# Delta loop of a small hybrid network: order of TensorE's work in a step, two-step loop body, identity products left out

## The reference, cut to what matters

```
def step(S, xs):
    qc, kc, vc, bc = xs
    kb = kc * bc[:, None]
    A = jnp.tril(kb @ kc.T, -1)
    U = solve_triangular(eye + A, vc * bc[:, None] - kb @ S, lower=True)
    o = qc @ S + jnp.tril(qc @ kc.T) @ U
    return (S + kc.T @ U, o)
```

## Time and profile before

| | us |
|---|---|
| median of three runs | 882.79 (877.17 to 887.01) |
| profiled execution, its own time | 882.23 |
| its span | 880.5 |
| TensorE busy | 637.1 (72%) |
| VectorE busy | 440.9 (50%) |
| ScalarE busy | 323.9 (37%) |
| GpSimd busy | 330.2 (38%) |
| mean granted TensorE clock | 0.832 |

### The profile page before, as it was taken

The page is one execution under the profiler, slowest core; times in us unless marked ns, Lnnn a source line. Parts: engine busy times, 40 slices in busy tenths (PEclk is TensorE's granted clock), DMA queues, the critical chain, the costliest instruction groups (busy, mean ns, idle before and its releaser), DMA issues. The chain is left out here.

```text
span 880.5 us, 38401 instructions
## 1 busy us (share of the span) xinstructions
PE 637.1 (72%) x15895; PEld 474.7 (54%) x15895; DVE 440.9 (50%) x1380; ACT 323.9 (37%) x743; POOL 330.2 (38%) x605
## 2 busy tenths in 40 slices
PE   5777105888886875368876189999832899999991
PEld 4565104777775774268876056767621354445551
DVE  3664350223232238826556036676538376776762
ACT  4554100122221213245554036455220556565651
POOL 3577302122121750345675654210021344646442
PEclk9888555599998577669999579999955899999995
DMA  3000222112210900544453111000005333333420
GB/s 104 8 15 21 79 86 69 38 66 71 72 65 22 330 26 1 99 137 131 152 158 106 48 38 28 17 4 4 4 1 99 101 98 100 108 99 106 100 83 1
DMA packets 62384, 63.72 MB, mean 72 GB/s; under 512 B 12432, under 2 KB 51903, under 8 KB 62017
## 3 DMA queue, kind: packets, MB, share of 16 engines
q1 hardware_dynamic: 57056, 52.35, 19.4%
q0 software_dynamic: 5216, 9.87, 5.3%
HBM read 20.50 MB, written 11.93 MB: 37 GB/s over the span
## 5 line engine op out<-in xcount | busy, mean ns | idle before, releaser
L1976 PE MATMUL e_psH<-wac,e_xT 128*64 x184 | 91.1, 618 | 1.0 <-ACT e_xT L2036 0.7
L1978 PE MATMUL e_psH<-e_up_w,e_xT 128*64 128x512 f32 x184 | 91.1, 618 | 0.0
L1921 POOL DMA_INDIRECT e_row<-xe_dram,e_read_at x46 | 44.6, 969 | 69.6 <-DVE spare L2167 44.3
L1926 POOL DMA_INDIRECT out<-spare,e_write_at x46 | 46.5, 1011 | 48.1 <-ACT spare L2053 37.8
L577 POOL TENSOR_TENSOR tb<-tinv,mb 128x128 f32<-128x128 f32 x64 | 24.3, 401 | 106.8 <-PE d_psY L594 106.8
L1321 ACT ACTIVATE e_hT<-e_psH,e_b 128x128 f32<-128x128 f32 x156 | 44.5, 369 | 39.2 <-PE e_psH L1277 39.2
L1233 POOL DMA_INDIRECT e_row<-xe_dram,e_read_at x39 | 38.7, 993 | 42.1 <-DVE spare L1392 27.7
L1277 PE MATMUL e_psH<-e_xT,e_up_w 128*128 128x128 f32 x312 | 45.5, 293 | 12.0 <-issue 9.9
L1997 PE MATMUL e_psY<-vb,e_hT 128*64 x368 | 50.9, 282 | 2.9 <-issue 2.9
L2160 DVE TENSOR_TENSOR e_h<-e_pre,e_psH 128x512 f32<-128x512 f32 x46 | 31.6, 688 | 42.4 <-ACT e_pre L2042 42.4
L2000 PE MATMUL e_psY<-e_down_w,e_hT 128*64 128x128 f32 x368 | 50.9, 282 | 0.0
(11 more groups left out here) (369 smaller groups left out, 1749.0 us busy)
## 6 DMA issues: line engine op xcount, KB each, us to landing
e_down_w<-vb SPq DMA_DIRECT2D x92, 128.0 KB, 2.0
e_up_w<-wa SPq DMA_DIRECT2D x39, 256.0 KB
xe_dram<-xe SPq DMA_DIRECT2D x2, 2080.0 KB, 12.4
vk_now<-vk SPq DMA_DIRECT2D x16, 192.0 KB
kq_now<-kq SPq DMA_DIRECT2D x16, 192.0 KB, 2.1
outs_dram<-spare SPq DMA_DIRECT2D x39, 64.0 KB
r<-in_L_attn_hidden_states SPq DMA_DIRECT2D x8, 256.0 KB, 3.1
gk_now<-gk SPq DMA_DIRECT2D x16, 128.0 KB, 2.0
```

What stands on the lines that cost most here:

```text
L1921: pool.indirect_dma_start(out=row[g % ROWS][:, :], out_offset=None, in_=x_dram, in_offset=bass.IndirectOffsetOnAxis(ap=read_at[:, g:g + 1] ...
L1926: pool.indirect_dma_start(out=out, out_offset=bass.IndirectOffsetOnAxis(ap=write_at[:, g:g + 1], axis=0), in_=z[:, g], in_offset=None, bou ...
L1976: nc.tensor.matmul(psH[g % 2][0:HALF, j], xT[g % 2][:, 0:HALF], wac[:, bass.ds(who[0][j], 1)].rearrange("p a f -> p (a f)"), start=True, s ...
L1978: mm = nc.tensor.matmul(psH[g % 2][HALF:P, j], xT[g % 2][:, HALF:P], up_w[g % 2][j][:, :], start=True, stop=True)
```

## The change

TensorE's step now holds three steps' work side by side: the solve of t + 1, the chunk products of t, in two halves (one for each sequence), and the scan of t - 1, whose pieces are parted into `states` and `outputs` and stand between all the rest. The solve of a step writes one bank throughout (`psY[i]`, `d_psZ` is gone), and steps alternate between two banks; `kq_now`, `mt` and `qe` have two buffers. As buffers alternate by the step's parity, the hardware loop has a body of two steps and seven passes; two steps' solves and one step's chunk products stand before it, step 15's chunk products and the rest of the scan behind it. The identity products are left out. ScalarE does the solve's copies of t + 1 before `on` of t, VectorE subtracts for `uw` first, and adds the outputs of a step one step later. The diff, cut:

```diff
-        vk_now, kq_now, gk_now = tmp("vk_now", [P, B * H, RW]), tmp("kq_now", [P, B * H, RW]), tmp("gk_now", [P, B * H, CH])
+        vk_now, gk_now = tmp("vk_now", [P, B * H, RW]), tmp("gk_now", [P, B * H, CH])
+        kq_now = [tmp(f"kq_now{i}", [P, B * H, RW]) for i in range(2)]
-        mt, qe = tmp("mt", [P, NC, B, CH]), tmp("qe", [P, B, NC, CH])
+        mt, qe = ([tmp(f"{n}{i}", s) for i in range(2)] for n, s in (("mt", [P, NC, B, CH]), ("qe", [P, B, NC, CH])))
-        solved_in, crossed_in = bank("d_psY", [P, 512]), bank("d_psZ", [P, 512])
-        psY, psZ = (t[:, 0:B * H * RW].rearrange("p (h c) -> p h c", c=RW) for t in (solved_in, crossed_in))
+        solve = [bank(f"d_psY{i}", [P, 512]) for i in range(2)]
+        psY = [t[:, 0:B * H * RW].rearrange("p (h c) -> p h c", c=RW) for t in solve]
...
-                    if t:
-                        sp.wait_ge(c_ps, t)
-                    sp.dma_start(kq_now[:, :, :].rearrange("p h c -> p (h c)"), kq[:, t].rearrange("p b h c -> p (b h c)")).then_inc(kq_in, 16)
+                    if t >= 2:
+                        sp.wait_ge(c_ps, t - 1)
+                    sp.dma_start(kq_now[t % 2][:, :, :].rearrange("p h c -> p (h c)"), kq[:, t].rearrange("p b h c -> p (b h c)")).then_inc(kq_in[t % 2], 16)
...
-                pool.memset(mt[:, :, :, :], 0.0).then_inc(const, 1)
+                for i in range(2):
+                    pool.memset(mt[i][:, :, :, :], 0.0).then_inc(const, 1)
...
-                half_words = sb["ident"][:, :].bitcast(BF16)[:, 0:P]
-
-                def full_array(bank):
-
-                    for _ in range(3):
-                        nc.tensor.matmul(bank[:, :], half_words, half_words, start=True, stop=True)
-
-                def first(t, start):
+                def first(t, i, start=False):
                     pe.wait_ge(vk_in, 16 * t + 16)
                     if not start:
-                        pe.wait_ge(uw_done, t)
+                        pe.wait_ge(uw_done, t - 1)
+                        pe.wait_ge(y_sb, t)
                     pe.wait_ge(expanded[0], t + 1)
                     pe.sem_inc(passed, 1)
-                    apply(0, lambda bh: vk_now[:, bh], psY, y_ps)
+                    apply(0, lambda bh: vk_now[:, bh], psY[i], y_ps)
...
+                def per_chunk(t, b, i, loads=0, start=False):
+
+                    if b == 0:
+                        pe.wait_ge(kq_in[i], loads)
+                        if not start:
+                            pe.wait_ge(on_done, t)
+                            pe.wait_ge(mt_done, t)
+                            pe.wait_ge(qe_done, t)
+                        pe.wait_ge(uw_done, t + 1)
+                        pe.sem_inc(passed, 1)
+                    for h in range(H):
...
+                def step(t, i, loads):
+
+                    j = 1 - i
+                    first(t + 1, j)
+                    states(t - 1, 0, j)
+                    per_chunk(t, 0, i, loads)
+
+                    outputs(t - 1, 0, j)
+                    states(t - 1, 1, j)
+                    across(t + 1, j)
+                    outputs(t - 1, 1, j)
+                    states(t - 1, 2, j)
+                    per_chunk(t, 1, i)
+                    outputs(t - 1, 2, j)
+                    states(t - 1, 3, j)
+
+                    second(t + 1, j)
+                    outputs(t - 1, 3, j)
+
+                pe.wait_ge(const, 1)
+                first(0, 0, True)
+                across(0, 0)
+                second(0, 0)
+                pe.wait_ge(const, 4)
+                pe.wait_ge(y_sb, 1)
+                pe.wait_ge(vk_in, 32)
+                pe.wait_ge(expanded[0], 2)
+                pe.sem_inc(passed, 1)
+                apply(0, lambda bh: vk_now[:, bh], psY[1], y_ps)
+                per_chunk(0, 0, 0, 16, True)
+                across(1, 1)
+                per_chunk(0, 1, 0)
+
+                second(1, 1)
+                with pe.Fori(0, PER // 2 - 1) as m:
+                    step(2 * m + 1, 1, 16 * m + 16)
+                    step(2 * m + 2, 0, 16 * m + 32)
+                t = PER - 1
+                states(t - 1, 0, 0)
+                per_chunk(t, 0, 1, 16 * PER // 2)
...
+                for c in range(2, NC):
+                    states(t - 1, c, 0)
+                    outputs(t - 1, c, 0)
                 for c in range(NC):
-                    scan(PER - 1, c)
+                    states(t, c, 1)
+                    outputs(t, c, 1)
...
+                solved(0)
+                crossed(0)
+                for t in range(PER):
+                    if t + 1 < PER:
+                        solved(t + 1)
+                        crossed(t + 1)
+                    own(t)
...
                 for t in range(PER + 1):
+                    if t < PER:
+                        remainders(t)
+                    if t >= 2:
+                        outputs(t - 2)
                     if t:
-                        state(t - 1, 0)
-                        state(t - 1, 1)
+                        for c in range(3):
+                            state(t - 1, c)
+                        if t == PER:
+                            state(t - 1, 3)
                     if t < PER:
...
                         if t:
-                            dve.wait_ge(c_ps, t)
...
+                            state(t - 1, 3)
+                        transfer(t)
+                outputs(PER - 1)
```

More of the change, by code:

```diff
@@ L611, in across, with second @@
                         for c in range(NC):
-                            mm = nc.tensor.matmul(psZ[row(c), bh], gk_now[key(c), bh], y0[key(c), bh * RW:(bh + 1) * RW], start=True, stop=True)
+                            mm = nc.tensor.matmul(psY[i][row(c), bh], gk_now[key(c), bh], y0[key(c), bh * RW:(bh + 1) * RW], start=True, stop=True)
                     mm.then_inc(z_ps, 1)
-                def second(t):
+                def second(t, i):
                     pe.wait_ge(expanded[1], t + 1)
@@ L618, in second @@
                     pe.sem_inc(passed, 1)
[L619 to L642, removed]
@@ L644, in scan @@
-                def scan(t, c):
+                    apply(1, lambda bh: zz[:, bh * RW:(bh + 1) * RW], psY[i], w_ps)
+                def per_chunk(t, b, i, loads=0, start=False):
[8 more added lines that the diff above has]
+                    for h in range(H):
+                        bh, at = b * H + h, (b * H + h) * RW
+                        for c in range(NC):
+                            nc.tensor.matmul(psC[row(h), c, b * P:b * P + RW], uw[row(c), at + DV:at + DV + CH], kq_now[i][row(c), bh],
+                                             start=True, stop=True)
+                        for c in range(NC):
+                            nc.tensor.matmul(psC[row(h), c, b * P + RW + CH:b * P + RW + 2 * CH], uw[row(c), at:at + DV], kq_now[i][row(c), bh, DK:RW],
+                                             start=True, stop=True)
+                        for c in range(NC):
+                            mm = nc.tensor.matmul(psC[row(h), c, b * P + RW:b * P + RW + CH], kq_now[i][row(c), bh, 0:CH], uw[row(c), at:at + DV],
+                                                  start=True, stop=True)
+                    if b == B - 1:
+                        mm.then_inc(c_ps, 1)
@@ L646, in scan, with states @@
+                def states(t, c, i):
                     pe.wait_ge(s_sb, NC * t + c + 1)
@@ L651, in scan, with outputs @@
                         for h in range(H):
-                            mm = nc.tensor.matmul(psS[row(h), b], mt[key(h), c, b], S[key(h), c, b], start=True, stop=True)
+                            mm = nc.tensor.matmul(psS[row(h), b], mt[i][key(h), c, b], S[key(h), c, b], start=True, stop=True)
                     mm.then_inc(s_ps, 1)
+                def outputs(t, c, i):
                     if c == 0:
@@ L659, in scan @@
                         for h in range(H):
-                            mm = nc.tensor.matmul(psO[row(h), b, row(c)], S[key(h), c, b], qe[key(h), b, c], start=True, stop=True)
+                            mm = nc.tensor.matmul(psO[row(h), b, row(c)], S[key(h), c, b], qe[i][key(h), b, c], start=True, stop=True)
                     mm.then_inc(o_ps, 1)
[L663 to L667, removed]
@@ new lines, in _ @@
+                second(1, 1)
[5 more added lines that the diff above has]
+                per_chunk(t, 0, 1, 16 * PER // 2)
+                outputs(t - 1, 0, 0)
+                states(t - 1, 1, 0)
+                per_chunk(t, 1, 1)
+                outputs(t - 1, 1, 0)
+                for c in range(2, NC):
+                    states(t - 1, c, 0)
+                    outputs(t - 1, c, 0)
@@ L680, in _, with solved @@
                 for c in range(NC):
[L681 removed]
+                    states(t, c, 1)
+                    outputs(t, c, 1)
             @block.scalar
             def _(act):
[L685 removed]
+                def solved(t):
                     act.wait_ge(y_ps, t + 1)
```

66 lines of the change are left out of this document (29 added, 37 removed).

## The result

The changed kernel took **1032.4 us**, median of four runs (1029.84 to 1033.42), against 881.67 for the kernel before, four runs with those of the same session: a ratio of 1.170, 95% interval 1.163 to 1.177. The forecast was 1009 within 908 to 1040, and named 1036 for ten blocks a pass.

A forecast was written before the change was run, and what follows sets the result against it. TensorE was taken to bound the kernel, refetched code to decide: start 17.7, seven passes at 34.1 and end 14.0 make 270.4 against 143.9 us, +126.5 on 882.5, so 1009 us; range 985 to 1040, down to 908 for partial refetch and clock.

The forecast's parts named there:

- Code size decides: Delta loop: a two-step body of about 2,090 TensorE instructions has its code blocks fetched again each pass; chance 0.55.
- The worst end: Loop passes: every block comes again in each pass, 34.1 us for two steps with nine blocks, 37.9 with ten.
- Nine blocks: Loop body: 8.2 blocks long, so 9 or 10 touched; nine taken for the sum, ten called nearly as likely.
- start 17.7: Code ahead of the loop: 96 more products, 1.5 blocks, add 5.7 us, so the start takes 17.7 us.
- end 14.0: Code behind the loop: 896 instructions, 3.5 blocks, 13.3 us and 0.7 for last waits, where 3.7 us are now.
- 3.79 us a block: TensorE's instruction fetch: time per 16 KB block, taken from the stops in the present loop's first pass.
- What the store holds: TensorE's instruction store: five blocks proven kept, lookahead of one; at best it holds the whole body, at worst nothing stays.
- Part of the body survives: Rival, loop passes: only two to four colliding blocks return per two-step pass, 926 to 972 us in all; chance 0.20.
- The steady step of 6.35: Steady loop step: 5.84 us busy plus half a back edge and some 0.2 gives 6.35 us, 1.5 less than 7.84.
- all stays: Rival, loop: the store holds nine or ten blocks, code fetched once, steps at 6.35 us, 883 us in all; chance 0.14.
- All stays, but the clock falls: Rival, loop: body held, but without identity products steps run at clock 0.50, about 8.8 us each, 910 us; chance 0.05.
- Covers and queues: Steady loop: other work covers the waits for `zz`, `y0` and `S`; load and engine queues cost nothing.

The follow-up runs named there:

- e1: Kernel before, its order and identity products kept, only the hardware loop given a body of two steps with step 15 behind it: 1020.4 us, ratio 1.160.
- e2: Changed kernel's new order without identity products, but in a loop body of one step with single buffers: 875.68 us, ratio 0.995 to the kernel before.
- e10: Changed kernel with twelve identity products run once ahead of the loop, nothing else altered: 1001.85 us, ratio 1.137 to the kernel before.
- e5: Kernel before with a two-step loop body, one kind of chunk products (L637) left out, eight blocks touched: 993.1 us, ratio 1.127.
- e4: Kernel before with a two-step loop body, two kinds of chunk products (L637, L640) left out, seven blocks touched: 887.95 us, ratio 1.008.
- e9: e8 with twelve identity products run once ahead of the loop: 859.11 us, ratio 0.972 to the kernel before; part of the work is left out.
- e8: Changed kernel with two of three kinds of chunk products (L635, L638) left out in the loop: 920.81 us, median of two, no ratio.
- e7: e2 with its loop over all sixteen steps, so no chunk product stands outside the loop: 872.1 us, ratio 0.990 to the kernel before.
- e3: Changed kernel with the nine identity products put back in each step: 1005.87 us, ratio 1.143 to the kernel before.
- e6: Kernel before without its nine identity products a step, nothing else changed: 895.37 us, ratio 1.015.

## Why the prediction was right, and where it was not

**Code size decides: right.** The worst end was taken, all blocks again in each pass, and 68 came in seven passes where "63 or more" was written. e1 and e2 part the two halves of the change: the body of two steps alone gives 1.160, the order alone 0.995.

**Nine blocks: wrong by one, and this is the whole miss in the number.** The prediction took nine and called ten nearly as likely. The eight weight loads after 189.92 show it was ten. Its terms against the trace: start 17.7 forecast, 15.9 measured; passes 265.3 with ten blocks (7 x 37.9), 265.1 measured; end 14.0, 13.3 measured. The sum with ten was 1036, the median is 1032.4. The start is the term that was mis-sized most, by 1.8 us. e10 shows the step from ten to nine directly, and lands at 1001.85 where the forecast for nine was 1009.

**3.79 us a block: right in size.** 265.1 us over 68 blocks are 3.90; e10 has 33.9/9 = 3.77, e5 32.5/9 = 3.6, e1 36.5/10 = 3.65. It is less in e5 and e1 because the block behind the loop's end and the first block of the next pass come beside each other, some 1.0 us apart. With that 1.0 taken off, and eight and nine blocks counted one after the other, it is 31.5/8 and 35.5/9, 3.9 in both.

**What the store holds: bounded in the prediction, shown now.** Seven blocks of a loop stay (e4, e9). With eight all are lost in each pass (e5) or in every second one (e8). In e8's held pass eight touched blocks are there together, and one more fetched makes all eight come again; in e9 one more beside seven is fetched without loss. That makes eight places, of which a loop can count on seven. That all are lost by one block too many is what the prediction's store that is filled in order does. The Trainium skill, Runtime: NRT & Kernel Launch, Instruction fetch mechanics, gives TensorE 128 KiB in blocks of 16 KiB, which is eight; these runs agree. The same section of the Trainium skill says that a taken branch whose target isn't in a window of two pages forces a fetch: here the trace disagrees, since the back edges of e4 and e9 reach over six blocks back (1,612 and 1,582 instructions) and the first block is not fetched again. And its "mostly hidden" for crossing a block is off by the whole result.

**Part of the body survives: excluded.** Neither the changed kernel nor e5 keeps a block from one pass to the next. What e8 does is the nearest to it, but it keeps all or nothing in turn, and needs a body that just touches eight. That its 920.81 us lies near that rival's 926 is chance, since e8 leaves work out.

**The steady step of 6.35: mis-sized.** e2 measured 6.98. Busy time was written as 5.84 and is 6.28, so taking 0.34 for each group of identity products off the busy time was too much: TensorE's busy records overlap, and the first group of the earlier trace rows ends at 192.49, when `across` has begun. That is 0.44 of the 0.63 us. The rest is mainly the back edge, which in e2 comes once a step (0.63) and not every second step. The number of the rival "all stays" (883) was not tested: no run has the two-step body held, and e2 and e7 (875.68 and 872.1) have a shorter first pass than it.

**All stays, but the clock falls: its reasoning was half right.** In the new order the clock stayed at 1.00 without identity products, once nothing stopped it (e2, e7). In the changed kernel it is 0.50 through all passes, but not for want of these products: e3 has them, and its passes run at 0.50 to 0.55 (windows 183:218 and 218:253). It goes with the stops, and no cost of its own shows there: 19.0 us of work lie under 38, and e3's nine-block passes (34.3 us, mean of six) are no shorter than those of e10 at 0.50 (33.9). But I carried this over to the old order, and expected e6 to be unchanged; it lost 1.5%. There TensorE has waits for ScalarE and VectorE in each pass, and the identity products stand in them. That these waits are why the two orders differ is likely but not shown: no run has the new order with such waits and without fetches.

**Covers and queues: right.** No wait on `zz`, `y0`, `S` or a transfer shows in the passes of the changed kernel, where the stops give much cover, and none of weight in e2, whose order differs a little (`outputs 3` stands before `second`, single buffers).

## What to carry to other kernels

Before a hardware loop's body is doubled, count the instructions of the engine (an fp32 product of small tiles is four here) and the blocks of 256 that the body touches from where it begins: up to seven were held; with eight all came again, in every pass or every second one; with nine and ten, all in every pass, at 3.6 to 3.9 us each. In the trace such a loop shows equal stops by "issue" inside groups of products, at the same places in each pass, and a count of instruction transfers that grows with the passes. A better order is worth having if it fits in the loop as it was: the same idea in a body of one step wins 0.5% (e2) to 1% (e7).

## What the runs showed of the hardware that was not expected

- The block fetched ahead counts: it takes one of the eight places, and with eight blocks in the body nothing (e5) or every second pass (e8) is held; e4, with seven, and e5 are 105 us apart.
- Where a loop starts matters as much as how long it is: 24 instructions that run once were worth 30.5 us in the medians and 26.5 between the profiled executions (e10), and the end of the alternation in e8.
- A block of which only eight weight loads are used costs a stop of 2.51 us of its own, no less than a full one.
- The granted clock can alternate within a steady loop (0.93 and 0.67 in stretches of 8.6 us, e6), at a price of 0.8 to 2.2% of the whole kernel.
